# A fused attention and expert kernel on Trainium2: the maximum's scores in six wide steps, both pair selections ahead of y, and two small jobs moved between engines

## What is computed

```python
x = x + attn(layernorm(x))      # 16 heads of 8, one shared k and v, causal softmax, projection
x = x + ffn(layernorm(x))

# ffn: product-key mixture of experts
xn  = rmsnorm(x) * gamma
sim = einsum('pbnhd,hkpd->pbnhk', (xn @ wq.T), keys)     # 2 sides, 8 heads, 32 keys
sx, ix = top_k(sim[0], 16); sy, iy = top_k(sim[1], 16)
scores, pk = top_k(sx[..., :, None] + sy[..., None, :], 16)   # best 16 of the sums
h   = gelu(xn @ down[expert]) * softmax(scores)
out = sum over heads and experts of h * up[expert]
```

## Time and profile before

| | |
|---|---|
| median of 3 runs | 955.2 us (953.35 to 955.55) |
| profiled execution | 956.12 us, its span 954.3 us |
| DVE busy | 788.2 us (83%) |
| PE busy | 729.4 us (76%), weight loads 466.6 us |
| ACT busy | 712.5 us (75%) |
| POOL busy | 635.9 us (67%) |
| granted TensorE clock, mean | 0.928 of full speed |
| DMA | 34 GB/s on average |

### The profile page before, as it was taken

One profiled execution on the slowest core, in us unless ns is written; L12 is line 12 of the kernel. 1 busy time (PEld: TensorE's weight loads), 2 busy tenths in 40 slices (PEclk: granted clock), 3 DMA queues, 4 the chain that ended last, 5 costly groups with the idle time before them and its releaser, 6 DMA issues.

```text
span 954.3 us, 21078 instructions
## 1 busy us (share of the span) xinstructions
PE 729.4 (76%) x6014; PEld 466.6 (49%) x6014; DVE 788.2 (83%) x2998; ACT 712.5 (75%) x1041; POOL 635.9 (67%) x371
## 2 busy tenths in 40 slices
PE   4574669697878878796978788787879797877464
PEld 3332326364555646463645556464646464554333
DVE  3217199898989899899989899998989898988776
ACT  1334498797979797988979797979889797958381
POOL 2012059595978869595949688695959595868561
PEclk9777799999999999999989999999999999988676
DMA  5321303021212204030212121030302121000000
GB/s 155 52 26 27 47 11 60 8 59 17 54 23 35 41 15 62 7 64 6 60 17 54 23 40 37 17 60 9 65 3 60 17 49 25 22 8 18 0 1 11
DMA packets 58160, 32.53 MB, mean 34 GB/s; under 512 B 5904, under 2 KB 57744, under 8 KB 57936
## 3 DMA queue, kind: packets, MB, share of 16 engines
q1 hardware_dynamic: 58128, 32.14, 18.7%
HBM read 19.93 MB, written 5.24 MB: 26 GB/s over the span
## 4 chain that ended last, share of the span: by engine, by line
issue 34%; PE 20%; POOL 18%; DVE 15%; ACT 8%; SPq 1%; DMA 1%; POOLq 1%; DVEq 0%; ACTq 0%
POOL acc L497 16%; DVE prob L1001 6%; PE score L1168 3%; DVE late_scores L853 3%; PE score L1292 3%; ACT late_scores L592 3%; PE misc L1268 2%; PE score L1305 2%; POOL pieces L484 2%; DVE halves L847 2%; ACT prob L698 2%; PE score L1171 2%; DVE acc L1013 1%; PE misc L1218 1%; PE score L1198 1%
## 5 line engine op out<-in xcount | busy, mean ns | idle before, releaser
L497 POOL TENSOR_TENSOR acc<-acc,prob 128x1024 f32<-128x1024 f32 x186 | 441.5, 2374 | 16.6 <-POOL acc L497 0.5
L1001 DVE SCALAR_TENSOR_TENSOR prob<-score,cut,prob 128x1024 f32<-128x1024 f32 x256 | 317.4, 1279 | 20.3 <-ACT prob L698 19.1
L698 ACT ACTIVATE prob<-score,neg_lse,unit 128x1024 f32<-128x1024 f32 x256 | 302.4, 1206 | 24.4 <-PE score L1292 21.1
L1292 PE MATMUL score<-sel,pieces_t 128*128 128x512 f16 x512 | 162.6, 402 | 70.5 <-DVE prob L1001 65.7
L497 POOL TENSOR_TENSOR acc<-prob 128x1024 f32<-128x1024 f32 x31 | 73.3, 2364 | 169.9 <-DVE prob L1001 169.9
L609 ACT ACTIVATE probs<-score 128x512 f32<-128x512 f32 x192 | 111.3, 597 | 46.7 <-PE score L1200 39.8
L1292 PEld LDWEIGHTS score<-sel,pieces_t 128*128 128x128 f16 x512 | 38.0, 101 | 138.4 <-DVE prob L1001 123.0
L1198 PE MATMUL score<-q_stack,k_stack 128*128 128x512 bf16 x192 | 76.2, 397 | 23.6 <-DMA q_stack<-max_t 16.1
L1168 PE MATMUL score<-k_ahead,q_ahead 128*128 128x256 bf16 (+1 forms) x512 | 80.5, 265 | 17.2 <-DMA q_ahead<-q_scratch 7.9
L1257 PE MATMUL score<-xn_kept,wdt 128*128 128x128 f32 x480 | 85.0, 278 | 4.4 <-DVE prob L1001 4.0
L592 ACT ACTIVATE halves<-score 128x512 bf16<-128x512 f32 x64 | 35.6, 594 | 69.2 <-PE score L1171 69.2
(11 more groups left out here) (131 smaller groups left out, 1468.7 us busy)
## 6 DMA issues: line engine op xcount, KB each, us to landing
q_ahead<-q_scratch SPq DMA_DIRECT2D x96, 64.0 KB
q_stack<-q_scratch SPq DMA_DIRECT2D x96, 64.0 KB
q_scratch<-qk_piece SPq DMA_DIRECT2D x16, 192.0 KB, 2.4
xin<-x SPq DMA_DIRECT2D x16, 128.0 KB, 4.1
xres<-x SPq DMA_DIRECT2D x16, 128.0 KB, 4.6
x_kept<-x SPq DMA_DIRECT2D x16, 128.0 KB, 2.0
out<-fin SPq DMA_DIRECT2D x16, 128.0 KB, 5.5
xn_kept<-xn_t SPq DMA_DIRECT2D x15, 128.0 KB, 2.0
```

The lines of the kernel that those rows point to most:

```text
L497: eng.tensor_tensor(acc[:, j, :], so_far, prob[:, j * FH + h, :], ALU.add).then_inc(acc_added, 1)
L698: eng.activation(prob[:, g, :], score[g % BUFS][:, :], ACT.Exp, bias=neg_lse[:, j, h:h + 1], scale=unit[:, :]).then_inc(prob_made, 1)
L1001: eng.scalar_tensor_tensor(prob[:, g, :], score[g % BUFS][:, :], cut[:, j, h:h + 1], prob[:, g, :], ALU.is_ge, ALU.mult).then_inc(prob_mas ...
L1292: ins = eng.matmul(score[g % BUFS][:, cols], pieces_t[:, j, h, :], sel[:, cols], start=True, stop=True)
```

## The change

It does five things. `scores_for_max` and `max_scores_back` work in six steps of 1024 columns, a whole PSUM buffer each, alternately in `score[1]` and `score[2]`; four of the six now stand ahead of `project_y` and `piece_transposes`. DVE does the selections of both tiles ahead of `make_y`; the subtraction of the best of tile 1 (`shift_best`) stays behind its `gate`. The tops of both tiles are copied into PSUM by one ScalarE instruction (`place_tops`) in place of two of DVE's, placed behind the seventh of the twelve `att_exp`. `sim_high_piece` moves from ScalarE to GpSimd, just ahead of each low piece. On PE and ACT `xn` comes ahead of `xhat` among the first pair scores. The diff, cut to its core:

```diff
@@ gpsimd
+            def sim_high_piece(b, j):
+                value = held(eng, at(sim_kept, b, j + 1))
...
+                eng.wait_ge(sim_kept, value)
...
+                eng.tensor_copy(pieces[:, j, :, 0, :], v).then_inc(sim_high, 1)
...
                 if a:
+                    sim_high_piece(i + 1, 0)
                     sim_low_piece(i + 1, 0)
+                    sim_high_piece(i + 1, 1)
                     sim_low_piece(i + 1, 1)
@@ scalar
+            def max_scores_back(b, w):
+                eng.wait_ge(max_scores, at(max_scores, b, w + 1))
...
+                src = score[1 + w % 2]
+                if w < 2:
+                    dst = halves[0][:, 8 * w:8 * w + 8, 0, :]
...
+                    dst = late_scores[:, 4 * (w - 2):4 * (w - 1), :].rearrange("p h k -> p (h k)")
...
+            def place_tops(b):
+                eng.wait_ge(key_step, at(key_step, b, SEARCHES))
+                eng.activation(misc[1][:, 0:TILES * P].rearrange("p (j h k) -> p j h k", j=TILES, h=FH),
+                               ranked[:, :, :, RANK_X:RANK_Y + RANKED], ACT.Copy).then_inc(top_placed, 1)
...
                 if a:
-                    for u in range(MAX_STEPS):
+                    for u in range(7):
+                        att_exp(i + 1, u)
+                if f:
+                    place_tops(i)
+                if a:
+                    for u in range(7, ATT_STEPS):
                         att_exp(i + 1, u)
...
                 if f:
                     best_exp(i, 0)
+                if m:
+                    max_scores_back(i + 2, 2)
+                    max_scores_back(i + 2, 3)
                 if a:
                     x2_back(i + 1)
...
                 if f:
                     pieces_back(i, 0)
                 if m:
+                    max_scores_back(i + 2, 4)
                 if f:
                     log_sum(i, 0)
                 if m:
+                    max_scores_back(i + 2, 5)
                 if f:
                     pieces_back(i, 1)
+                if a:
+                    xn_back(i + 1)
...
                     pair_probs(i, 0, 0)
                     best_exp(i, 1)
+                if p:
+                    xhat_back(i + 3)
+                if f:
                     pair_probs(i, 0, 1)
@@ vector
+            def select_keys(b):      # the MAX8 of both tiles, then the MATCH_REPLACE8 of both
...
             def sum_pairs(b, j):
-                eng.wait_ge(key_step, at(key_step, b, (j + 1) * KEY_STEPS))
-                placed = misc[1][:, 0:FH * 2 * RANKED].rearrange("p (h k) -> p h k", k=2 * RANKED)
-                eng.tensor_copy(placed, tops).then_inc(top_placed, 1)
+                eng.wait_ge(key_step, at(key_step, b, SEARCHES + FH * (j + 1)))
+                eng.wait_ge(top_placed, every(top_placed, b))
...
                 if f:
-                    select_keys(i, 0)
-                    select_keys(i, 1)
+                    select_keys(i)
                     sum_pairs(i, 0)
                     select_pairs(i, 0)
+                    shift_best(i, 0)
                     sum_pairs(i, 1)
+                    select_pairs(i, 1)
                 if a:
                     make_y(i + 1)
...
                     sum_best(i, 0)
-                    select_pairs(i, 1)
                 if d:
                     gate(i - 1, 1)
                 if f:
+                    shift_best(i, 1)
                     log_sum_exp(i, 0)
@@ tensor
+            def scores_for_max(b, w, d=False):
+                if w == 0:
+                    eng.wait_ge(ahead_in, every(ahead_in, b))
+                    if d:
+                        eng.wait_ge(act_made, every(act_made, b - 3))
+                elif w == 1:
                     if later(b):
                         eng.wait_ge(att_probs, at(att_probs, b, 0))
+                else:
+                    eng.wait_ge(max_kept, at(max_kept, b, w - 1))
+                for u in (2 * w, 2 * w + 1):
+                    bank = score[1 + w % 2][:, (u % 2) * BANK:(u % 2 + 1) * BANK]
...
+                if j == 1 and m:      # in acc_transposes
+                    eng.wait_ge(max_kept, at(max_kept, b + 3, WIDE_STEPS - 1))
...
+                if m:
+                    scores_for_max(i + 2, 0, d)
+                    scores_for_max(i + 2, 1)
                 if d:
                     acc_transposes(i - 1, 0)
                 if m:
+                    scores_for_max(i + 2, 2)
+                    scores_for_max(i + 2, 3)
...
                 if m:
+                    scores_for_max(i + 2, 4)
+                    scores_for_max(i + 2, 5)
                 if f:
                     piece_transposes(i, 1, piece_t_made, at(piece_t_made, i, 1))
...
                     pair_scores(i, 0, 0, a, m)
+                if a:
+                    xn_transpose(i + 1, piece_t_made, i)
+                if f:
+                    pair_scores(i, 0, 1, a, m)
                 if p:
                     xhat_transpose(i + 3, x2_made, i + 1)
```

More of the change, by code:

```diff
@@ L39 @@
 BANK = 512
-MAX_STEPS = 12
+ATT_STEPS = 12
+WIDE_STEPS = 6
 BUFS = 3
@@ L649, in sim_back @@
                 eng.activation(sim[:, j, :], misc[1 - j][:, :], ACT.Copy).then_inc(sim_kept, 1)
[L651 to L656, removed]
             def pieces_back(b, j):
@@ L708, in prologue @@
                 xhat_back(1)
-                for u in range(MAX_STEPS):
-                    max_scores_back(0, u)
+                for w in range(WIDE_STEPS):
+                    max_scores_back(0, w)
                 qk_high_piece(1)
@@ L714, in prologue @@
                 max_back(0)
-                for u in range(MAX_STEPS):
+                for u in range(ATT_STEPS):
                     att_exp(0, u)
@@ L718, in prologue @@
                 invert_sums(0)
-                for u in range(4):
-                    max_scores_back(1, u)
+                for w in range(2):
+                    max_scores_back(1, w)
                 x2_back(0)
-                for u in range(4, MAX_STEPS):
-                    max_scores_back(1, u)
+                for w in range(2, WIDE_STEPS):
+                    max_scores_back(1, w)
                 xn_back(0)
@@ L908, in sum_pairs @@
-            def sum_pairs(b, j):
-                eng.wait_ge(key_step, at(key_step, b, (j + 1) * KEY_STEPS))
-                tops = ranked[:, j, :, RANK_X:RANK_Y + RANKED]
-                tops_x = tops[:, :, 0:RANKED]
-                placed = misc[1][:, 0:FH * 2 * RANKED].rearrange("p (h k) -> p h k", k=2 * RANKED)
-                eng.tensor_copy(placed, tops).then_inc(top_placed, 1)
-                eng.wait_ge(top_placed, at(top_placed, b, j + 1))
-                tops = placed
+            def select_keys(b):
+                for j in range(TILES):
+                    value = held(eng, at(sim_kept, b, j + 1))
+                    eng.wait_ge(setup_dve, 1)
+                    eng.wait_ge(sim_kept, value)
+                    for col, a in ((RANK_Y, 1), (RANK_X, 0)):
+                        for h in range(FH):
+                            keys_of = sim[:, j, (2 * h + a) * KEYS:(2 * h + a + 1) * KEYS]
+                            eng.max(ranked[:, j, h, col:col + RANKED], keys_of).then_inc(key_step, 1)
+                for j in range(TILES):
+                    value = held(eng, at(key_step, b, j * LISTS + FH))
+                    eng.wait_ge(setup_dve, 1)
+                    eng.wait_ge(key_step, value)
+                    for h in range(FH):
+                        ys_of = sim[:, j, (2 * h + 1) * KEYS:(2 * h + 2) * KEYS]
+                        eng.match_replace(left[:, j, h, :], ranked[:, j, h, RANK_Y:RANK_Y + RANKED], ys_of,
+                                          LOWEST).then_inc(key_step, 1)
@@ L1337, in prologue @@
                 keep_busy(score[1], 40)
-                for u in range(MAX_STEPS):
-                    scores_for_max(0, u)
+                for w in range(WIDE_STEPS):
+                    scores_for_max(0, w)
                 project_qkv(1, xhat_t_made, 1)
@@ L1351, in prologue @@
                 weigh_values(0, 1, max_t_made, 0)
-                for u in range(4):
-                    scores_for_max(1, u)
+                for w in range(2):
+                    scores_for_max(1, w)
                 project_y(0, xhat_t_made, 2)
                 eng.wait_ge(setup_done, 2)
-                for u in range(4, MAX_STEPS):
-                    scores_for_max(1, u)
+                for w in range(2, WIDE_STEPS):
+                    scores_for_max(1, w)
                 xn_transpose(0, y_t_made, 0)
@@ L1398, in iteration @@
                 if m:
-                    for u in range(2, 7):
-                        scores_for_max(i + 2, u)
+                    scores_for_max(i + 2, 4)
+                    scores_for_max(i + 2, 5)
                 if f:
                     piece_transposes(i, 1, piece_t_made, at(piece_t_made, i, 1))
-                if m:
-                    for u in range(7, 10):
```

(6 more changed lines are left out.)

102 lines of the change are left out of this document (31 added, 71 removed).

## The result

The changed kernel takes 927.69 us, median of 4 runs (925.1 to 930.18), against 954.52 us of the kernel before in the same session: a ratio of 0.9719, 95% interval 0.9689 to 0.9749, so 2.8% faster. Forecast were 931 us and a range of 919 to 949. The profiled execution has a span of 926.1 us.

A forecast was written before the change was run, and what follows sets the result against it. The POOL loop was taken as the bound: 34.95 + (0.87 + 1.13 + 3.9) + 0.2 + 0.8 + 8.57 = 50.4 us; 13 periods plus 2.6 give 657.8, 22.6 less. With the ends, -24.0: 931 us, range 919 to 949.

The forecast's parts named there:

- The POOL loop: POOL's adds, the path to DVE's gate of tile 1, then on to the next first add: period 50.4 us.
- The statistics: On DVE, delayed by the earlier selection, they still end before PE's turned sums: covered by 0.7 us.
- The price of the high piece: One POOL copy ahead of each low piece: 0.87 us, between near bounds of 0.58 and 1.15 us.
- The chain behind the low piece: From the end of low piece 0 to the gate of tile 1: 3.9 us, before 7.1 us.
- The wide steps: Four of six stand ahead of the pieces and fill PE's wait; ACT's step 4 takes 1.02 us.
- PE's wait for the pieces: PE's idle time for POOL's low pieces shrinks from 2.76 to about 1.3 us.
- The selection ahead of y: On DVE, 3.75 us of work pass ahead of y and delay the statistics; covered, by 0.7 us.
- The meeting with xhat: Behind the gate, DVE's shift_best, log sum and fold collide with POOL's xhat: 0.8 us a period.
- The clock: Drops of TensorE's clock cost 7.3 us in all before; a third, 2.6 us, is kept.
- The ends: Prologue and iteration 0 together give -2.0 us, the last two iterations +0.6 us.

The follow-up runs named there:

- dve_pad: The changed kernel with two more DVE memsets of 384 columns, behind masks 3 and 5 of tile 1: 927.94 us, 0.9695 of the kernel before.
- tops_on_dve: The changed kernel with the tops copied into PSUM by DVE again, one copy per tile, without place_tops: 929.91 us, 0.9727 of the kernel before.
- high_on_act: The changed kernel with the high pieces back on ScalarE, behind pair_probs 3 and 5: 922.5 us, 0.9645 of the kernel before.
- split_back: The changed kernel with each wide step copied back by two ACT instructions of 512 columns: 927.52 us, 0.9707 of the kernel before.
- steps_behind: The changed kernel with wide steps 2 and 3 back behind the first pieces on PE and ACT: 944.89 us, 0.9908 of the kernel before.
- select_late: The changed kernel with select_pairs of tile 1 back behind sum_best(0), so behind y: 954.98 us, 0.9988 of the kernel before.
- before_select_first: The kernel before with only select_pairs of tile 1 moved ahead of y: 986.8 us, 1.0321 of the kernel before.
- xhat_cut: The changed kernel with both POOL xhat instructions cut to 2 of 128 columns past the fourth batch: 917.2 us, 0.9588 of the kernel before.

## Why the prediction was right

**The POOL loop.** Right, and its terms as well: 34.95 predicted and 34.94 measured for the adds, 5.9 and 5.93 to the gate, 9.57 and 9.38 from there. The statistics were ready before the turned sums, as forecast: DVE idles 0.89 us ahead of the gate, where 0.7 was said. `dve_pad` and `tops_on_dve` show that 0.6 us more of DVE's work in a period changes nothing, `high_on_act` that one copy off the loop is one copy off the period.

**The price of the high piece.** Predicted 0.87 us, measured 0.61 and 0.69 from start to start: nearest the lower bound, that of the memset. The 769 ns that the prediction quotes from the Trainium skill is above it as well; the measurement decides. The chain behind the low piece took 4.14 in place of 3.9; the two misses cancel.

**The wide steps.** The 1.02 us taken from the activation's row was the duration (median 1.023). That their place and not their width carries a gain holds; `split_back` and `steps_behind` part the two. PE's wait for the pieces shrank more than said, from 2.76 to 0.74 us and not to 1.3.

**The selection ahead of y.** Here a step failed. It was costed at nothing, "covered", and the text didn't see that it is what the steps ahead of y depend on. In the changed kernel DVE fills with it the time in which PE and ACT do the steps; `select_late` shows 4.0 us of waits without it. Costing the edit against the kernel before (+2.3 us a period on average, by `before_select_first`) or against the rest of the change (-1.9, by `select_late`) gives opposite signs. The sum came out right since it was made for the whole and the selection was walked through in its place; as an account of the parts it would have been wrong.

**The meeting with xhat.** Predicted 0.8, measured 0.6 in the rows and 0.67 in `xhat_cut`, and as forecast in the log sum and the fold. The Trainium skill's "SBUF — State Buffer", "Who interferes with whom", is borne out: two SBUF inputs on DVE (the log sum, the fold) against a reading instruction on POOL (L446, L450), each waiting for the other's end. L900 took only 0.16 us, as L897 had already waited until both pieces were through (423.12 against 423.09). L897 itself is a case that the rule, as the prediction tells it, doesn't cover: it has one input from SBUF and two constants, and took 0.92 us in place of 0.17. And not every POOL instruction holds DVE up: `shifted` (L978) started beside POOL's small power (L443, 128x2) and took its usual 0.28.

**The clock.** This term came out by luck. 2.6 us were kept for drops among 13 like periods; between iterations 1 and 12 they cost nothing, though the clock did fall in five of them. Instead the period of iteration 0 alone was 2.8 us longer than the others, which the sum didn't look at apart (the 7.3 us of before hold 1.9 of it). The last period was 0.7 shorter, for want of xhat, which wasn't in the sum either.

**The ends:** -2.3 and -1.0 against -2.0 and +0.6. In all 28.2 us were saved in the profiled execution (954.3 - 926.1) where 24.0 were forecast; of the 4.2 more, 2.3 come from the 13 periods, 0.3 and 1.6 from the ends.

## What to carry to other kernels

Look for one event that each engine's loop must pass, take the distance of its occurrences, and add up one round; a term that is not in this sum pays nothing, however busy its engine is. Price the parts of a reordering together as well as alone: work moved ahead on one engine is only a gain if the engine that waits for it has something else to do meanwhile, and either part may be worthless or do harm without the other. Look as well at what the moved instruction will stand beside on the other engines. And once the loop is known, its idle stretch is the place for what stands in the path: POOL's idle time ahead of its first add took both high pieces for nothing.

## What was not expected of the hardware

A POOL copy of 512 fp32 columns to fp16 takes 0.61 us, 1.19 ns a column, about what its memset takes (1.14) and half of what an instruction with two operands takes. The wait between DVE and POOL doesn't scale with the work: 4 columns on POOL took 1.07 us (`xhat_cut`) and 2 on DVE 0.92 (L897) while the other was in a long instruction.
